# Two graph layers and two feed-forward layers on one core: on TensorE, the placing products of a group of edges stand in front of the own products of the group two ahead

## What is computed

```python
# graph layer 0: 4 heads, O = 64, src and dst as the attention uses them
feats = einsum('nd,hdo->hno', x, Ws) + bs[:, None, :]
score = a_s[:, src] + a_d[:, dst] + aw_e[:, None] * elem[None, :] + ab[:, None]
w = exp(-relu(score / 20.0))
pooled = segment_sum(w * feats[:, dst], src)
out = pooled / segment_sum(w, src)[:, :, None]

# graph layer 1: 200 relations, one weight per edge
score = h[src] @ w_src + h[dst] @ w_dst + rel_emb[etype] @ w_rel
alpha = exp(leaky_relu(score))
alpha = alpha / sum(alpha, axis=1)
agg = segment_sum((h[src] + rel_emb[etype]) @ weight_neighbor * alpha, dst)
node_repr = relu(agg) + loop_message      # h @ loop_weight, or another where no edge comes in
```

## Time and profile before

| | us |
|---|---|
| median of 3 runs | 2502.88 (2497.65 to 2503.34) |
| profiled execution, its own time | 2481.36 |
| its span, first to last instruction | 2479.6 |
| layer 0's edges, window 270 to 949 | 679.00 |
| layer 1's edges, window 1556 to 2270 | 714.00 |

### The profile page before, as it was taken

The page is one execution under the profiler, slowest core; times in us unless marked ns, Lnnn a source line. Parts: engine busy times, 40 slices in busy tenths (PEclk is TensorE's granted clock), DMA queues, the critical chain, the costliest instruction groups (busy, mean ns, idle before and its releaser), DMA issues. The chain is left out here.

```text
span 2479.6 us, 40282 instructions
## 1 busy us (share of the span) xinstructions
PE 1639.9 (66%) x9301; PEld 1175.0 (47%) x9301; DVE 1690.6 (68%) x4231; ACT 1080.0 (44%) x2994; POOL 1264.8 (51%) x1217
## 2 busy tenths in 40 slices
PE   0678466565666665289999956466676666766378
PEld 0576244343444444289999954233333333333266
DVE  8997766666666667677778646567777777777811
ACT  0474334443333343212222226676676676664321
POOL 0387566666666660126666610655666565652042
PEclk9889667667666666599999977566677667777689
DMA  3014444444444443289999962555665565663331
GB/s 101 2 5 68 152 107 108 109 108 110 109 108 110 107 98 67 65 281 279 301 303 303 305 213 77 172 164 160 167 165 165 161 167 162 167 169 49 91 87 22
DMA packets 212676, 351.09 MB, mean 142 GB/s; under 512 B 45840, under 2 KB 123980, under 8 KB 212588
## 3 DMA queue, kind: packets, MB, share of 16 engines
q0 software_dynamic: 75616, 167.60, 27.1%
q1 hardware_dynamic: 136972, 182.41, 23.9%
HBM read 318.55 MB, written 31.34 MB: 141 GB/s over the span
## 5 line engine op out<-in xcount | busy, mean ns | idle before, releaser
L1164 POOL DMA_INDIRECT e_rows<-table,e_gidx x880 | 846.5, 962 | 525.2 <-issue 233.1
L1227 DVE TENSOR_TENSOR acc<-acc,e_psO 128x260 f32 (+1 forms) x880 | 463.5, 527 | 274.9 <-DMA edge_rows<-row_out 156.6
L1437 PE MATMUL e_psO<-e_rows,e_oh 128*128 128x260 f32 x880 | 374.5, 594 | 233.4 <-DVE acc L1227 206.0
L1437 PEld LDWEIGHTS e_psO<-e_rows,e_oh 128*128 128x128 f32 x880 | 236.3, 290 | 314.6 <-DVE acc L1227 209.3
L2277 PE MATMUL e_psO<-e_rows,e_oh 128*128 128x456 bf16 x440 | 225.1, 512 | 95.3 <-DVE acc L1227 84.1
L1318 PE MATMUL e_psA<-e_own_of_unit,e_ohT 128*128 (+2 forms) x880 | 104.1, 184 | 188.2 <-issue 80.4
L1318 PEld LDWEIGHTS e_psA<-e_own_of_unit,e_ohT 128*128 128x128 bf16 x880 | 82.0, 103 | 274.6 <-issue 263.3
L1406 ACT ACTIVATE e_rows<-e_psA 128x16 f32<-128x16 f32 x110 | 20.3, 184 | 399.5 <-DVE e_psA L1397 300.8
L788 POOL DMA_INDIRECT records<-ordered,s_chunk x68 | 119.1, 1752 | 110.7 <-DVE s_chunk L615 80.9
L2179 ACT ACTIVATE away<-iota_b,etype 128x200 bf16<-128x200 bf16 x440 | 165.3, 446 | 0.0
L2237 DVE TENSOR_SCALAR e_oh<-iota_b,seg,inverse 128x128 bf16<-128x128 bf16 x440 | 117.9, 337 | 69.3 <-issue 57.7
(11 more groups left out here) (444 smaller groups left out, 3669.6 us busy)
## 6 DMA issues: line engine op xcount, KB each, us to landing
hot_run<-in_L_ffn_w_dram SPq DMA_DIRECT2D x107, 512.0 KB
XN<-in_L_ffn_w_dram SPq DMA_DIRECT2D x85, 512.0 KB
e_edge_row<-edge_rows SPq DMA_DIRECT2D x110, 256.0 KB
e_edge_row<-edge_rows SPq DMA_DIRECT2D x110, 128.0 KB
e_rows<-table,e_gidx POOLq DMA_INDIRECT x880
table<-frow SPq DMA_DIRECT2D x25, 192.5 KB
table<-chunk_steps SPq DMA_DIRECT2D x25, 130.0 KB, 2.2
normed_rows<-Z SPq DMA_DIRECT2D x5, 642.5 KB
```

Of the source, the lines that this page charges most:

```text
L1164: pool.indirect_dma_start(out=rows[:, r, t, 0:width], out_offset=None, in_=table, in_offset=bass.IndirectOffsetOnAxis(ap=gidx[:, r, t:t + ...
L1227: v.tensor_tensor(d, d, psO[:, units * (r % (4 // units)) + j, 0:accw], ALU.add).then_inc(S["added"], 1)
L1437: return pe.matmul(out[:, 0:A0], oh[:, r, t, :], rows[:, r, t, :], start=start, stop=stop)
```

## The change

In PE's `step` the two blocks change places. Within a step the placing products of group s-1 come first, and then the own products of s+1. Waits and posts stay with their products; no other engine's code changes. Since lines move, the own products are at L1333, L1336 and L1337 in the changed kernel; L1437 and L2277 to L2279 keep their numbers.

```diff
                 def step(s, dyn):
                     nxt, last = (locate(s, dyn, d) for d in (1, -1))
+                    if last is not None:
+                        g, q, r = last
+                        pe.wait_ge(S["payload"], g + 1)
+                        if post.get("spread"):
+                            pe.wait_ge(S["weight_kept"], g + 1)
+
+                        pe.wait_ge(S["counted" if l else "oh_ready"], g + 1)
+                        for t in range(TPG):
...
+                        ins.then_inc(S["summed"], 1)
                     if nxt is not None:
                         g, q, r = nxt
                         pe.wait_ge(S["ohT_ready"], g + 1)
...
                         ins.then_inc(S["own_e"], 1)
-                    if last is not None:
-                        g, q, r = last
-                        pe.wait_ge(S["payload"], g + 1)
...
-                        ins.then_inc(S["summed"], 1)
                 pipeline(pe, 1, 1, step, post.get("pe_besides", ()))
```

More of the change, by code:

```diff
@@ L1304, in step @@
                     nxt, last = (locate(s, dyn, d) for d in (1, -1))
+                    if last is not None:
[5 more added lines that the diff above has]
+                        for t in range(TPG):
+                            u = t // tpu
+                            if t % tpu == 0:
+                                back(pe, S["added"], g, 4 // units, per=units, extra=u + 1 - units)
+                            ins = post["product"](pe, psO[:, units * (r % (4 // units)) + u, :], oh, rows, r, t,
+                                                  t % tpu == 0, t % tpu == tpu - 1)
+                        ins.then_inc(S["summed"], 1)
                     if nxt is not None:
```

## The result

The changed kernel takes 2668.14 us (2664.61 to 2671.33, 4 runs) beside 2502.74 us (2497.65 to 2503.34, 4 runs) for the kernel before: 1.0665 times, 95% interval 1.0646 to 1.0685, so 165 us slower. The forecast was 2506 us with a range up to 2565. Its profiled execution has a span of 2669.6 us. That is 190 us over the span of the kernel before, 25 more than the medians are apart, mostly since the profiled run of the kernel before was 0.9% under its median.

What follows compares the result with a forecast made beforehand. POOL's issue and the landing of its last fetch were taken to set the pace. Parts (1) and (2) gave 0, part (3) +3 us, on the median of 2502.88: 2506 us, range 2470 to 2565.

Steps and rivals of the forecast that it cites:

- Part (1): On PE, placing no longer stands behind the own products' wait for the one-hots: at most 8 us earlier, worth 0.
- Part (2): Own products posted behind placing: DVE's late-group add 0.20 us later in layer 0, 0.25 in layer 1; covered, worth 0.
- the 0.54 us of POOL's spare time: Slack before the prompt `summed` would delay POOL's fifth fetch; the first shift uses 0.20 us of it.
- Part (3): Starts and ends of both layers' edge phases, where no fetch is queued: 0.6 to 0.8 us uncovered each, +3 us.
- The slip: Rival: prompt `summed` turns late, +1.12 us a group in layer 0, up to +123 us; layer 1 at most 20; chance 0.16.
- The shift: Rival: POOL's fifth fetch, or DVE in layer 1, moves with the later adds: +10 to +35 us; chance 0.17.
- the gain: Rival: new order removes what makes posts late, POOL's stops shrink: -8 to -64 us; chance 0.20.
- The signs named beforehand: Layer 0: 12.3 us for two groups, eight fetches, one 2.5 us stop; POOL's stops near 48 and 54 by layer.

Runs made afterwards that it cites:

- adds-first run: Changed kernel with DVE's four adds all ahead of its own reduce, both layers: 2522.18 us, ratio 1.0068, where posts come late; 2344.37 us, ratio 1.0544, where none does.

## Why the prediction was wrong

**What bounds the kernel** was read rightly, for the chips with late posts: the pace is set by POOL's fetches and by a post that is seen only after the last of them is issued; with plain loads the kernel is 390 us faster. Its sentence that the late `summed` becomes visible "when the queued fetches have landed" fits its own rows, but is not shown in general: with the own products ahead of the last tile the post was seen while they still moved. What no profile of one chip could show is that this is no fixed property: on another chip the kernel before takes 2223 us, and there POOL doesn't stop for PE in the profile of the kernel with one layer changed.

**Part (1)**, earlier placing worth 0: no run speaks against it. Where no post was late neither layer's new order gained anything (0.9999, 0.9991).

**Part (2)** holds the step that failed: "so `own_e` of group s comes just behind `summed` of s-2", priced at the length of the reduce and the products. The wait for `own_e` was taken to end with the wait for `summed`. That came from three places at which the reduce and the add came 0.20 us apart, all in layer 0. There it held: the reduce stands 0.20 us ahead of its add, and POOL starts 0.75 us behind the release. The prompt add moved by 4.85 - 4.47 = 0.38 us against the release, not 0.8, so the 0.54 us of POOL's spare time were enough, and layer 0's order didn't show in the time (2675.52 us with the old order there, 2677.39 with the new). In layer 1 two posts 0.5 us apart met with different fates: `summed` at 1914.56 was prompt, `own_e` at 1915.07 held for 7.6 us. Priced at +0.25 us a group, it cost 5.18 - 0.75 = 4.4 us in such a period, and the 186 us by which POOL's stops grew are 42 of them. The adds-first run shows this wait as the cause: without it 2522 us in place of 2677. Why `own_e` was held in layer 1 and not in layer 0 (654.30) stays open.

In the old order `own_e` was posted ahead of the placing, and the post that was held was the one that released DVE and POOL together (1890.83 and the like: placing ended at 1887.82, and the update of its `summed` stands at 1890.70), so that both lost only the delay of that one post. The prediction saw that DVE and POOL "had both waited for the same `summed`" and did not ask what comes of it if the held post is one for which only DVE waits, while POOL needs the next one.

**Part (3)**, 3 us at the ends: not resolved.

**The rivals.** The slip had the right kind of cause, a post that the change makes late for a reason that no row showed, and the right warning that it decides for a whole phase. It had the wrong post (`summed`, not `own_e`), the wrong layer, and a price that ended at 2643 us with a chance of 0.16. Its question, what makes one post prompt and the next late, should have been put to every post that the change moves, in both layers. The shift and the gain did not happen.

**The signs named beforehand** held for layer 0. In layer 1 POOL's stops are as many as forecast (54), but the own reduce idles 6.9 us and POOL 7.0 us in the period shown, where a stop of 2.5 us was named.

## What to carry to other kernels

When an instruction moves behind another that ends a step, list who waits for each of the two posts, and ask what happens if the first is seen and the second is not: an in-order engine that stands on the second holds up all that the first has released. A post that is seen late costs only its own delay as long as it releases every engine that is idle by then; it costs a whole chain if the engine that feeds the others waits for the next post. And measure a small change of order on more than one chip where the profile shows idle time that no instruction explains.

## What the runs showed of the hardware

- TensorE's posts can be seen several microseconds late while POOL's indirect fetches are in flight: 7.6 us in the changed kernel's layer 1 (1915.07 to 1922.68), 4.9 us in the earlier trace rows. In the periods shown they come 2.1 to 2.8 us after the last fetch was issued (1906.70 to 1908.80, 1919.94 to 1922.68, 644.05 to 646.81), and not with the end of the data: behind 1908.80 the DMA engines are still 0.81 busy at 179 GB/s, behind 646.81 they move nothing. A post of DVE was not late in such a stretch: in the trace of the kernel before DVE ends a one-hot at 630.34, 7.3 us after the first fetch of a stream (623.02), and the own products that wait for it begin at 630.84.
- In these runs it took POOL's indirect fetches. Plain loads by SP at 206 GB/s didn't do it, and fetches of a quarter or a fifth of the bytes did it as well as whole ones (2669 against 2653 us).
- No fixed time after the first fetch of a stream parts prompt posts from late ones. In the changed kernel `summed` was prompt 3.5 us after it in layer 1 (1911.08 to 1914.56) and `own_e` 3.9 us after it in layer 0 (650.43 to 654.30), while in layer 1 `own_e` was held 4.0 us after it; but with the own products ahead of the last tile `own_e` was held 3.0 us after it, when three fetches were issued (1902.95 to 1905.91). What decides stays open.
- It depends on the chip, or on a lasting condition of it: in the runs of the result and on two chips of the experiments the kernel before took 2477 to 2505 us, with the stops in both its profiles; on one chip 2223 us, without them as far as the changed kernels' profiles tell. Why, and by what way the fetches hold the posts, stays open.
- No version beat the kernel before on the chips with late posts; the best with the gather in it was adds first, 2522 us against 2505.
